# Subtracting the low halves of queries and keys on VectorE in place of GpSimd, in a six-layer perceiver kernel

## What is computed

```
q = l2norm(q) * sqrt(SCALE); k = l2norm(k) * sqrt(SCALE)
sim = q @ k.T ; attn = softmax(sim) ; out = layernorm((attn @ v) @ wo) + x
```

## Time and profile before

| | |
|---|---|
| median of 3 executions | 2590.43 us (2587.82 to 2591.18) |
| the profiled execution: its own time | 2594.97 us |
| its span, first to last instruction | 2593.3 us |
| mean granted TensorE clock | 0.974 of full speed |
| busy: PE, DVE, ACT, POOL | 2487.2, 2220.2, 2057.0, 604.3 us |
| POOL subtractions, 24 each for sa, ca, kv | 114.3 us (48) and 51.3 us (24) |
| one round in the middle | 99.85 us, each like the next |

### The profile page before, as it was taken

One profiled execution on the slowest core, in us unless ns is written; L12 is line 12 of the kernel. 1 busy time (PEld: TensorE's weight loads), 2 busy tenths in 40 slices (PEclk: granted clock), 3 DMA queues, 4 the chain that ended last, 5 costly groups with the idle time before them and its releaser, 6 DMA issues.

```text
span 2593.3 us, 38049 instructions
## 1 busy us (share of the span) xinstructions
PE 2487.2 (96%) x12652; PEld 1528.1 (59%) x12652; DVE 2220.2 (86%) x4411; ACT 2057.0 (79%) x3973; POOL 604.3 (23%) x392
## 2 busy tenths in 40 slices
PE   4799999999999999999999999999999999999986
PEld 2456656656656566666566566566566565665565
DVE  6689898898898898898898988988988988989874
ACT  2588888888888888888888888888888888888742
POOL 3312312213213213123123122122132131231000
PEclk7799999999999999999999999999999999999985
DMA  3000010001001001001001001001001000000000
GB/s 129 25 9 17 25 35 19 25 8 40 13 13 53 9 17 47 9 17 53 9 17 46 9 17 52 9 17 47 2 24 36 17 25 30 17 9 26 1 1 4
DMA packets 16573, 63.56 MB, mean 25 GB/s; under 512 B 2241, under 2 KB 7410, under 8 KB 11642
## 3 DMA queue, kind: packets, MB, share of 16 engines
q1 hardware_dynamic: 16378, 61.13, 7.3%
HBM read 48.25 MB, written 0.29 MB: 19 GB/s over the span
## 4 chain that ended last, share of the span: by engine, by line
PE 51%; ACT 18%; DVE 17%; issue 10%; POOL 3%; DMA 0%; ACTq 0%; SPq 0%; DVEq 0%; POOLq 0%
PE psS L1049 14%; PE psO L1097 8%; ACT P L884 8%; PE psO L1098 7%; PE psO L1100 7%; ACT PH L881 6%; DVE PL L634 4%; PE psL L1143 3%; PE psL L1154 2%; PE psL L1049 2%; ACT qraw L903 1%; DVE back_x L707 1%; ACT QT L899 1%; POOL back_rstd L420 1%; POOL front_rstd L420 1%
## 5 line engine op out<-in xcount | busy, mean ns | idle before, releaser
L881 ACT ACTIVATE PH<-psS 128x512 fp32r<-128x512 f32 x1536 | 1010.4, 658 | 168.8 <-PE psS L1049 150.1
L634 DVE TENSOR_TENSOR PL<-P,PH 128x512 fp32r<-128x512 f32 x1536 | 1038.6, 712 | 92.9 <-ACT P L884 83.1
L884 ACT ACTIVATE P<-psS 128x512 f32<-128x512 f32 x1536 | 1010.5, 658 | 109.9 <-DVE PL L634 109.8
L1049 PE MATMUL psS<-QT,KT 128*128 128x512 f16 x3072 | 926.6, 383 | 0.8 <-ACT P L884 0.8
L1097 PE MATMUL psO<-PH,V 128*128 128x512 f32 x1536 | 875.5, 570 | 0.0
L1100 PE MATMUL psO<-PL,V 128*128 128x512 f32 x1536 | 606.8, 395 | 0.0
L1098 PE MATMUL psO<-PH,VL 128*64 128x512 f32 x1536 | 605.5, 394 | 0.0
L1049 PEld LDWEIGHTS psS<-QT,KT 128*128 128x128 f16 x3072 | 216.2, 100 | 368.7 <-issue 288.6
L1097 PEld LDWEIGHTS psO<-PH,V 128*128 128x128 f32 x1536 | 291.9, 190 | 177.6 <-ACT PH L881 9.8
L1100 PEld LDWEIGHTS psO<-PL,V 128*128 128x128 f32 x1536 | 288.0, 187 | 151.7 <-DVE PL L634 0.6
L420 POOL TENSOR_TENSOR rn<-ssc,neghalf 128x16 f32<-128x16 f32 (+2 forms) x73 | 240.5, 3294 | 347.7 <-DVE ssc L569 265.9
(11 more groups left out here) (363 smaller groups left out, 2857.2 us busy)
## 6 DMA issues: line engine op xcount, KB each, us to landing
ctx_sb<-ctxT SPq DMA_DIRECT2D x24, 1024.0 KB, 4.8
KT<-KT SPq DMA_DIRECT2D x48, 256.0 KB, 3.5
W<-wpack SPq DMA_DIRECT2D x6, 1280.0 KB, 5.4
W<-wpack SPq DMA_DIRECT2D x6, 1088.0 KB, 7.3
W<-wpack SPq DMA_DIRECT2D x6, 576.0 KB, 5.7
KT<-biasM SPq DMA_DIRECT2D x1, 1024.0 KB
W<-tail_w SPq DMA_DIRECT2D x1, 832.0 KB
P<-biasW SPq DMA_DIRECT2D x1, 512.0 KB
```

Source lines behind the costliest of these rows:

```text
L634: nc_v.tensor_tensor(PL[:, here, :], P[:, t % PSLOTS, :], PH[:, here, :], ALU.subtract).then_inc(sem("p_lo"), 1)
L881: nc_a.activation(PH[:, t % HSLOTS, :], bank, ACT.Exp, scale=SIM_SCALE).then_inc(sem("p_hi"), 1)
L884: nc_a.activation(P[:, t % PSLOTS, :], bank, ACT.Exp, scale=SIM_SCALE).then_inc(sem("ca_exp"), 1)
L1049: ins = mm(bank, keys[part], q, start=(part == 0), stop=(part == 1))
```

## The change

The helper `low` moves from POOL's block to DVE's and issues the same subtraction of the same operands, behind the same wait and with the same count of the same semaphore. `f_low_sa` stands at step 13 of DVE's table behind `t0_gain` (a stage of the tail, absent in most rounds), `f_klow` at step 22 and `f_low_ca` at step 59. POOL's table loses the three. The tables of PE and ACT are as before.

```diff
-            13: ["f_null", "f_V3", "t0_norm", "b_out", "t0_gain"], 14: ["u_norm"],
+            13: ["f_null", "f_V3", "t0_norm", "b_out", "t0_gain", "f_low_sa"], 14: ["u_norm"],
...
-            22: ["s_ready", "f_sp0", "f_sp1", "t0_key3"], 23: ["u_cell0", "t0_mask2", "t1_gain"],
+            22: ["s_ready", "f_sp0", "f_sp1", "t0_key3", "f_klow"], 23: ["u_cell0", "t0_mask2", "t1_gain"],
...
-            59: ["t1_cols", "t1_res"], 60: ["e_scale2", "t1_z"], 61: ["u_res", "f_nv"], 64: ["b_end"],
+            59: ["t1_cols", "t1_res", "f_low_ca"], 60: ["e_scale2", "t1_z"], 61: ["u_res", "f_nv"], 64: ["b_end"],
...
-            0: ["f_sa"], 1: ["s_null"], 5: ["t0_fin", "f_rot", "f_sa_q"], 7: ["u_fin"], 8: ["s_mask"], 9: ["f_low_sa"],
-            11: ["t0_y"], 12: ["u_y", "t0_y2", "b_out"], 13: ["b_ff"], 14: ["u_y2", "f_kv"], 16: ["t1_fin"],
-            20: ["t1_y", "t1_y2"], 23: ["f_klow"], 26: ["f_out"], 35: ["f_ca"], 36: ["s_rows"], 40: ["f_ca_q"],
-            48: ["f_low_ca"], 54: ["t0_z"], 56: ["t1_z"], 60: ["u_z"], 65: ["v_fin", "v_y", "v_y2", "v_z"],
+            0: ["f_sa"], 1: ["s_null"], 5: ["t0_fin", "f_rot", "f_sa_q"], 7: ["u_fin"], 8: ["s_mask"], 11: ["t0_y"],
+            12: ["u_y", "t0_y2", "b_out"], 13: ["b_ff"], 14: ["u_y2", "f_kv"], 16: ["t1_fin"], 20: ["t1_y", "t1_y2"],
+            26: ["f_out"], 35: ["f_ca"], 36: ["s_rows"], 40: ["f_ca_q"], 54: ["t0_z"], 56: ["t1_z"], 60: ["u_z"],
+            65: ["v_fin", "v_y", "v_y2", "v_z"],
...
-            def low(tag, half, whole, high):
-                def stage(n, par):
-
-                    pool.wait_ge(sem(tag + "_hi"), n + 1)
-                    nc.gpsimd.tensor_tensor(half, whole, high, ALU.subtract).then_inc(sem(tag + "_lo"), 1)
-                return stage
...
+            def low(tag, half, whole, high):
+                def stage(n, par):
+
+                    dve.wait_ge(sem(tag + "_hi"), n + 1)
+                    nc_v.tensor_tensor(half, whole, high, ALU.subtract).then_inc(sem(tag + "_lo"), 1)
+                return stage
...
+            stages["f_low_sa"] = low("sa", qs[:, :, 1, :], qn[:], qs[:, :, 0, :])
+            stages["f_low_ca"] = low("ca", qs[:, 0:H, 1, :], qn[:, 0:H, :], qs[:, 0:H, 0, :])
+            stages["f_klow"] = low("kv", ks[:, :, 1, :], kn[:], ks[:, :, 0, :])
```

More of the change, by code:

```diff
@@ L470, in _ @@
                 "f_rot": f_rot, "s_null": s_null, "s_rows": s_rows, "s_mask": s_mask,
-                "f_low_sa": low("sa", qs[:, :, 1, :], qn[:], qs[:, :, 0, :]),
-                "f_low_ca": low("ca", qs[:, 0:H, 1, :], qn[:, 0:H, :], qs[:, 0:H, 0, :]),
-                "f_klow": low("kv", ks[:, :, 1, :], kn[:], ks[:, :, 0, :]),
                 "f_sa": row_power(front, "sa"), "f_sa_q": head_power("sa", 17), "f_out": row_power(front, "sao"),
```

## The result

The changed kernel takes **2626.52 us** (median of four runs, 2622.52 to 2629.31), the kernel before 2589.89 beside it (2587.82 to 2591.18): a ratio of 1.0140, 95% interval 1.0126 to 1.0153. It is 36.6 us slower. The profiled execution took 2624.19 us, its span 2622.1.

What follows compares the result with a forecast made beforehand. The bound was taken to change within a round: DVE until about 520 us, then PE without a gap to 566, DVE nearly as full. 23 rounds x 1.84 less 2.2 gave +40 us: 2630 us, range 2606 to 2650.

Steps and rivals of the forecast that it cites:

- Prices: Each subtraction on DVE was priced like the scaling to unit length: about 1.2 us for 1088 columns, 1.15 for 1024.
- f_low_sa: After `b_out`: DVE gets 1.26 us of hold back and spends 1.2, net 0; PE reaches `b_turn` 0.9 us later.
- f_klow: After `f_sp1`: DVE stands 1.35 us for ACT's line 956, then subtracts for 1.15; 2.5 us, with PL behind it.
- What it becomes at f_out: At `f_out` DVE, 2.5 us late less 0.66 of waits, is 1.84 us late: the cost of a round.
- The later of the two counts: At `f_out`, of PE's 1.4 us and DVE's 1.84 us lateness, only the later counts: 1.84 us a round.
- Scores and projection: PE's scores wait for a bank and its output projection follows: PE 1.4 us late, including 0.9 from before `b_turn`.
- f_low_ca: At step 59: 0.35 us of waiting and 1.15 of work, 0.9 back on PL, rest covered at `b_end`; cost 0.
- First round: PE's two waits for POOL's subtractions in the first round shrink by 1.1 us each: -2.2 us.
- Sum: 23 rounds x 1.84 = 42.3 us, less 2.2: +40 us, a median of 2630 us.
- PE alone: Rival: buffers swallow DVE's lateness after `f_klow`; only PE's 0.9 us before `b_turn` stays: +18.5, 2609 us; chance 0.12.
- Costs add: Rival: line 707's hold stays (2658 us), or PE's 0.9 and DVE's 1.84 come one after the other (2651); chance 0.15.
- Faster: Rival: a 0.6 us subtraction ends `b_out` and it 0.65 us earlier, `f_klow`'s cost staying within waits: 2574 us; chance 0.05.

Runs made afterwards that it cites:

- only_sa: Kernel before with only the self-attention queries' subtraction moved to DVE, behind `b_out`; POOL keeps the others: 2606.21 us, ratio 1.0070.
- sa_early: Kernel before with only the self-attention queries' subtraction moved to DVE, ahead of `b_out` at the same step: 2588.78 us, ratio 0.9995.
- the three single kernels: Kernel before with one subtraction each moved to DVE: keys' 2628.26 us, self-attention queries' 2606.21, cross-attention queries' 2588.94.
- only_ca: Kernel before with only the cross-attention queries' subtraction moved to DVE, at step 59: 2588.94 us, ratio 0.9998.
- only_klow: Kernel before with only the keys' subtraction moved to DVE, at step 22: 2628.26 us against 2591.11, ratio 1.0153.
- klow_24: Changed kernel with `f_klow` two steps later, at step 24 behind `f_spread0`: 2608.98 us, ratio 1.0068.
- slots_dve: Kernel before with line 707's copy and `f_null` at step 3 (first round's `f_null` unmoved), both queries' subtractions on DVE, `f_low_sa` ahead of `b_out`: 2570.16 us, ratio 0.9911.
- copy_early: Kernel before, all subtractions on POOL, with only the copy of line 707 moved one step earlier, to step 12: 2604.55 us, ratio 1.0057.
- pool_again: Changed kernel with POOL repeating the self-attention queries' subtraction in two instructions into an unread tile, PE waiting for it too: 2647.47 us, ratio 1.0216.

## Why the prediction was right, step by step

The forecast was 2630 us, 2606 to 2650; 2626.52 was measured.

- **Prices.** Right: 1.22 to 1.29 us for the subtraction on DVE; I had taken 1.15 to 1.2 of the engine, and the instruction behind it starts 1.14 to 1.21 us later. The Trainium skill, page "GPSIMD Engine Reference", section "Engine selection", has GpSimd at about twice VectorE's time with two inputs; the trace agrees (2.49 against 1.28 us), and the kernel is slower with the faster engine all the same.
- **f_low_sa.** Right, twice. DVE lost nothing (522.21 against 522.28), since the hold of 1.26 us came back, and `b_turn` was 0.91 us late where I had 0.9. only_sa gives +0.86 a round for it by itself. That it is the place is shown by sa_early.
- **f_klow.** Right in mechanism, slightly too large. The wait is 1.22 us and not 1.35: I had taken POOL's start at 533.48 for the end of it, and DVE starts at 535.63, which is 533.35 by the round before. PL behind it is 2.37 late and not 2.5.
- **What it becomes at f_out.** "1.84 us a round" measured 1.65. The waits of 0.16, 0.20 and 0.30 were given back as I had them (2.37 - 1.65 = 0.72, forecast 0.66); the rest of the difference is the 0.13 of the term above. "The later of the two counts" is what the three single kernels show: 37, 15 and 0 against 36.6 for all.
- **Scores and projection.** PE was to be 1.4 late; it was 1.29 at the scores and 1.43 at the projection.
- **f_low_ca.** Right: 0, as only_ca shows. PL that took 1.62 us beside POOL takes 0.69, and the wait at `b_end` went down from 0.73 to about 0.17 (3.8 us in 22 times). So POOL held not only the copy but this product too: in the earlier trace rows it ends at 586.54, 0.54 behind POOL's subtraction.
- **First round.** I had -2.2 us. PE's two waits for the subtractions there shrank about as I had it, from 7.3 to 6.3 us in only_sa and from 9.2 to 8.3 in only_ca. The stretch as a whole is 3.6 shorter in the profile after; it varies by 4.5 between kernels, so what the term was worth in the time is neither confirmed nor refuted.
- **Sum.** Rounds too long by 0.19 each, 4 us in all, and the forecast was 3.5 high. That the total is so close is partly luck: the two ends of the kernel moved by 3.6 and 3.1 us between the two profiles, and the sum had one term of -2.2 for them.

The rival "PE alone" fell with only_klow, where PE's transposes stand at their old place and a round still costs 1.76 more. It needs DVE's lateness to be swallowed down to less than PE's, and klow_24 shows that this happens when the keys' subtraction no longer waits. "Costs add" fell with the single kernels. "Faster" needed the hold to be worth more than the new wait. It pays nothing on that side: sa_early takes the hold away and gains nothing, because DVE puts a subtraction of the same length in its place. The gain of 22 us appears when the copy and `f_null` leave DVE's way to `b_out`, even with the subtraction still in it: from the scaling to the first norm of `b_out` it is 5.27 us in the kernel before (510.66 to 515.93), 5.20 in sa_early and 4.41 in slots_dve (506.45 to 510.86). No run moves `f_null` alone, so how much of the gain needs the copy moved as well is not shown.

Two expectations of mine failed for one reason. For copy_early I looked at the instruction that was held and not at the next one that could be, and for pool_again I placed POOL's two instructions by their length without asking which gap the copy would fall into. Where two engines share something, the start times to a tenth of a microsecond decide. What stays open is why the first round and the end of the kernel vary by several us, and why the same pause is followed by the lower clock in some rounds and not in others.

## What to carry to other kernels

Work moved to a faster engine must be priced by its place in that engine's queue: what it stands behind, what stands behind it, and which engine is the late one at the next meeting. Here the same three subtractions on the same engine cost 36.6 us or 7.7 us (2597.66 against 2589.93) by their places alone. Where two engines are late at one meeting the larger lateness counts, so removing one of them is worth only the difference; and an instruction that is mysteriously long beside another engine's work should be moved together with its neighbours that could be held in its stead.

## What the runs showed of the hardware

- A DVE copy of 64 columns in fp16, from SBUF to SBUF, took 2.25 us when it started 0.12 us after POOL's subtraction (copy_early), and 0.19 us when it started 0.14 us ahead (the kernel before) or 0.02 us after it (line 650 in copy_early). A 128x128 fp32 copy was held in the same way (1.49 and 1.50 us against 0.22), until POOL's instruction ended. A PL product, a subtraction of two 32-bit tensors in SBUF, that started at 584.92, beside POOL's until 586.00, took 1.62 us against 0.69. The cast and the subtraction that read PSUM just ahead of line 707 took 0.42 us each beside POOL's subtraction, as they do without it.
- In pool_again such a copy started 0.15 us before the second of two POOL instructions in a row, and ran in 0.22 us.
- After a pause of PE of 2.74 us the granted clock went to its lower level for some 3 us in 18 of 22 rounds, although PE worked without a gap by then; after one of 2.07 us it did so in 4 of 22, after one of 1.51 us in none of 22. A round in which it fell was 1.0 to 1.4 us longer than one with the same pause in which it did not.
